# Order of the first loads in a four-layer kernel: x of batch 0 with the first four tiles of weights, the other batches of x last

## What is computed

```python
qk = x @ qk_w.T
vg = x @ vg_w.T
q, k = (qk[..., :KEY_DIM], qk[..., KEY_DIM:])
v, g_out = (vg[..., :VAL_DIM], vg[..., VAL_DIM:])
q = _causal_dwconv_silu(q, q_conv_w)   # the same for k and v
beta = _sigmoid(x @ b_w.T + b_bias + beta_bias) * 2.0
g = -jnp.exp(A_log) * jax.nn.softplus(x @ a_w.T + dt_bias)
o = _gated_delta_rule(q, k, v, g, beta)
o = o * jax.lax.rsqrt(jnp.mean(o * o, axis=-1, keepdims=True) + eps)
o = o * silu(g_out)
x = _layernorm(x + o @ o_w.T)
```

## Time and profile before

| | us |
|---|---|
| median of three runs | 2795.45 |
| lowest and highest | 2789.07, 2799.66 |
| the profiled execution, its time | 2794.95 |
| its span, first to last instruction | 2793.2 |
| TensorE busy | 2512.8 (90%) |
| VectorE busy | 1856.1 (66%) |
| GpSimd busy | 1384.0 (50%) |
| ScalarE busy | 1258.0 (45%) |

### The profile page before, as it was taken

How to read it: one execution, slowest core, us unless ns; L and a number is a source line. 1 busy time by engine, 2 the same in 40 slices (tenths; PEclk the granted TensorE clock), 3 DMA queues, 4 the chain that set the end, 5 groups by cost and what they waited for, 6 DMA issues and landing times.

```text
span 2793.2 us, 33262 instructions
## 1 busy us (share of the span) xinstructions
PE 2512.8 (90%) x11786; PEld 1467.7 (53%) x11786; DVE 1856.1 (66%) x2240; ACT 1258.0 (45%) x1997; POOL 1384.0 (50%) x741
## 2 busy tenths in 40 slices
PE   5999939999989999989678899989989888999998
PEld 2455624444677888855233333333433333677776
DVE  4678875554555666665579789889978888722223
ACT  3443205531223666434456655764665452334333
POOL 0222338860040000241299999999999996122221
PEclk9999759998989999999889899999999999999999
DMA  6443683432053777641275676587587565100000
GB/s 223 140 121 102 87 112 88 95 94 105 12 216 128 256 261 259 208 125 51 84 186 160 173 210 182 162 202 217 170 204 213 174 194 191 46 1 16 15 1 31
DMA packets 278967, 384.98 MB, mean 138 GB/s; under 512 B 127104, under 2 KB 148608, under 8 KB 271392
## 3 DMA queue, kind: packets, MB, share of 16 engines
q1 hardware_dynamic: 268944, 335.77, 41.4%
q0 software_dynamic: 9296, 38.80, 5.7%
q10 hardware_dynamic: 576, 8.39, 0.7%
HBM read 312.91 MB, written 59.51 MB: 133 GB/s over the span
## 4 chain that ended last, share of the span: by engine, by line
PE 55%; POOL 15%; DVE 11%; issue 6%; SPq 5%; DMA 4%; ACT 4%; another core or an unknown queue 0%; PEldq 0%; ACTq 0%; DVEq 0%; POOLq 0%; PEld 0%
POOL arena L786 8%; PE psum L2036 8%; POOL arena L792 5%; PE psum L1983 4%; PE psum L2217 4%; PE psum L2218 4%; PE psum L2832 4%; SPq L2293 4%; PE psum L3019 2%; PE psum L2190 2%; PE psum L2191 2%; PE psum L483 2%; PE psum L2823 1%; PE psum L1879 1%; PE psum L2082 1%
## 5 line engine op out<-in xcount | busy, mean ns | idle before, releaser
L786 POOL TENSOR_TENSOR arena<-arena 128x1024 f32<-128x1024 f32 x256 | 626.3, 2466 | 130.9 <-DVE arena L1551 82.7
L2036 PE MATMUL psum<-arena,cst 128*128 128x512 f32 x1024 | 507.4, 631 | 101.4 <-POOL arena L792 90.4
L1090 ACT ACTIVATE psum<-arena,negA 128x512 f32<-128x512 f32 x512 | 333.4, 682 | 319.0 <-DVE arena L1566 276.4
L2036 PEld LDWEIGHTS psum<-arena,cst 128*128 128x128 f32 x1024 | 189.3, 197 | 400.7 <-issue 215.2
L1566 DVE TENSOR_TENSOR_SCAN arena<-psum,arena 128x512 f32<-128x512 f32 x256 | 310.6, 1213 | 58.8 <-ACT psum L1090 37.6
L1566 DVE TENSOR_TENSOR_SCAN psum<-psum,arena 128x512 f32<-128x512 f32 x256 | 298.7, 1212 | 57.8 <-POOL arena L786 55.0
L792 POOL TENSOR_TENSOR arena<-arena 128x1024 f32<-128x1024 f32 x128 | 312.7, 2443 | 3.0 <-DVE arena L1566 3.0
L840 POOL TENSOR_TENSOR arena<-arena 128x512 f32<-128x512 f32 x64 | 92.3, 1442 | 324.2 <-ACT arena L1214 299.2
L1983 PE MATMUL psum<-arena 128*128 128x512 f32 x512 | 231.8, 596 | 1.3 <-PE psum L1983 0.8
L2381 POOL TENSOR_TENSOR arena<-arena,cst 128x512 f32<-128x512 f32 x64 | 76.3, 1216 | 270.2 <-DVE arena L2685 178.9
L2369 POOL TENSOR_TENSOR arena<-arena,cst 128x1024 f32<-128x1024 f32 x96 | 184.8, 1953 | 43.2 <-PE psum L2933 25.9
(11 more groups left out here) (373 smaller groups left out, 5000.7 us busy)
## 6 DMA issues: line engine op xcount, KB each, us to landing
arena<-bc_scr SPq DMA_DIRECT2D x256, 512.0 KB, 5.4
arena<-w_exp SPq DMA_DIRECT2D x23, 1408.0 KB, 6.1
arena<-in_gu SPq DMA_DIRECT2D x48, 512.0 KB, 4.6
arena<-in_inw SPq DMA_DIRECT2D x32, 512.0 KB, 4.4
arena<-in_dn SPq DMA_DIRECT2D x31, 512.0 KB, 6.9
x_scr<-arena SPq DMA_DIRECT2D x19, 512.0 KB, 5.9
arena<-in_x SPq DMA_DIRECT2D x8, 1024.0 KB, 11.6
w_exp<-in_gu SPq DMA_DIRECT2D x16, 512.0 KB, 7.1
```

The source lines that it names most:

```text
L786: nc.gpsimd.tensor_tensor(dB[:, k % 4], du[:, j:j + 2], BC[:, k % RING, 0].unsqueeze(1).broadcast_to([P, 2, T]), ALU.mult).then_inc(s["db_ ...
L1090: nc.scalar.activation(psum[:, bank], dt[:, b % 2, j + t], ACT.Exp, scale=negA2[:, at:at + 1]).then_inc(s["da_ok"], 1)
L2036: ins = mm(psum[:, t], ident, dB[:, k % 4, t], start=False, stop=(n == NS - 1), skip_group_check=True)
```

## The change

SP issues x of batch 0 right behind the constants, then the three parts of the weights. x of batch 0 and the first part of the weights raise `xload`, the other two parts raise `wload`. SP then waits for the constants and issues x of batches 1 to 3, which raise `consts`, up to 64. TensorE waits for `xload` at 32 ahead of batch 0, for `wload` at 32 ahead of tile 4 of batch 0, and for `consts` at 64 ahead of the later batches and of their gate rows. The bases of the semaphores' second names follow.

```diff
-                ("stt_ok", "std_ok", B), ("vd_ok", "rinv_ok", B), ("ab_in2", "xload", 64), ("ab_in3", "wload", 48),
+                ("stt_ok", "std_ok", B), ("vd_ok", "rinv_ok", B), ("ab_in2", "xload", 32), ("ab_in3", "wload", 32),
...
-                ("w_in0", "m_in", 128 * B), ("w_in1", "t_out", 128 * B), ("xr_in0", "xload", 64 + 96),
-                ("xr_in1", "wload", 48 + 96), ("tg_in0", "ab_in0", 96), ("tg_in1", "ab_in1", 96), ("tg_in2", "v_in1", 128),
+                ("w_in0", "m_in", 128 * B), ("w_in1", "t_out", 128 * B), ("xr_in0", "xload", 32 + 96),
+                ("xr_in1", "wload", 32 + 96), ("tg_in0", "ab_in0", 96), ("tg_in1", "ab_in1", 96), ("tg_in2", "v_in1", 128),
...
         @block.sync
         def _(sp):
             sp.dma_start(cst[:], a["cst"]).then_inc(s["consts"], 16)
-            for c in range(3):
-                sp.dma_start(wproj[:, 4 * c:4 * c + 4], a["wproj"][:, 4 * c:4 * c + 4]).then_inc(s["wload"], 16)
-            for b in range(B):
-                sp.dma_start(xin[:, :, b * T:(b + 1) * T], a["x"][:, :, b * T:(b + 1) * T]).then_inc(s["xload"], 16)
+            sp.dma_start(xin[:, :, 0:T], a["x"][:, :, 0:T]).then_inc(s["xload"], 16)
+            for c, done in enumerate(("xload", "wload", "wload")):
+                sp.dma_start(wproj[:, 4 * c:4 * c + 4], a["wproj"][:, 4 * c:4 * c + 4]).then_inc(s[done], 16)
+            sp.wait_ge(s["consts"], 16)
+            for b in range(1, B):
+                sp.dma_start(xin[:, :, b * T:(b + 1) * T], a["x"][:, :, b * T:(b + 1) * T]).then_inc(s["consts"], 16)
             sp.wait_ge(s["ini"], 5)
...
             pe.wait_ge(s["consts"], 16)
-            pe.wait_ge(s["wload"], 48)
...
             for b in range(B):
-                pe.wait_ge(s["xload"], 64)
+                pe.wait_ge(s["consts"], 16 * B) if b else pe.wait_ge(s["xload"], 32)
                 xb = xin[:, :, b * T:(b + 1) * T]
 
                 def proj(c, bank, done):
+                    if b == 0 and c == 4:
+                        pe.wait_ge(s["wload"], 32)
...
                     pe.wait_ge(s["ini"], 8)
+                    if b:
+                        pe.wait_ge(s["consts"], 16 * B)
                     ring_wait(pe, "r", b, 0)
```

## The result

The changed kernel takes 2780.01 us in the median of 11 runs (2772.44 to 2789.80), the kernel before 2792.85 in the median of 11 (2784.93 to 2800.83). The ratio is 0.9955, 95% interval 0.9938 to 0.9973: 12.6 us less, between 7.5 and 17.3. That is within 0.5% by a little. 2780.01 lies 1.5 us under the forecast of 2781.5, and that closeness is partly luck: the kernel before came out 2.6 us lower over 11 runs (2792.85) than over the three that the forecast started from (2795.45), and the gain 1.1 to 1.3 us smaller than 13.9.

The account below looks back on a forecast made before the run. TensorE's chain bounds the kernel, its first matmul idle 25.1 us until the last load of x. The earlier start gives 13.9 us, all other terms 0: 2795.45 less 13.9 is 2781.5 us, range 2775.5 to 2788.

Parts of the forecast that it names:

- Rival A: The forecast itself: all 13.9 us gained at TensorE's first matmul reach the end of the kernel; 78%.
- Part 1: TensorE's first wait: with loads reordered, gate rows start at 11.2 instead of 25.07 us, gaining 13.9 (12.7 to 14.3).
- Parts 2 and 3: Tile 4's weight wait is met with 14 us spare; SP's wait leaves late x 50 us spare; no cost.
- Part 4: Added wait instructions on TensorE: all met beside matmuls in flight, between 0 and 0.3 us, taken as 0.
- Part 5: TensorE's clock: low-clock spells, about 2 us and one a batch, follow idle stretches and move along at unchanged cost.
- B: Queued early loads are served side by side, so TensorE starts at 16.1; 8.9 us gained, 2786.5; 3%.
- C: Low-clock spells fall differently over the attention stage: two more give 2785.5 (7%), two fewer 2777.5 (8%).
- D and E: Unmoved later work, such as SP's zero writes, absorbs the gain (2795, 2%); or batch 1's x arrives late (2809, 2%).

Follow-up runs that it names:

- weights ahead of x: Changed kernel's waits kept, but all three parts of the weights issued before x of batch 0; ratio 0.9971 to the kernel before.
- first weights, x: Changed kernel with only the first part of the weights issued before x of batch 0; ratio 0.9952 to the kernel before.
- gate rows on x alone, nine matmuls ahead: Kernel whose gate rows wait only for x of batch 0, plus nine unused matmuls on the constants before that wait; ratio 0.9960 to the kernel before.
- small constants first: Against the changed kernel: last 380 constant columns load before x, the rest after the first weights; gate rows wait only for x; 2787.49 us, ratio 0.9939.
- The first experiment: Changed kernel's load order kept, but TensorE again waits for all eight loads before its first matmul; 2795.55 us, ratio 1.0007 to the kernel before.

## Why the prediction was right

The kernels in the order of their start. The third column is 1 - (25.07 - start) / 2793, the start alone carried one for one to the end:

| kernel | first gate matmul | by the start | measured ratio |
|---|---|---|---|
| all waits back | 25.14 | 1.0000 | 1.0007 (0.9996 to 1.0017) |
| weights ahead of x | 16.34 | 0.9969 | 0.9971 (0.9960 to 0.9982) |
| changed | 12.54 | 0.9955 | 0.9955 (0.9938 to 0.9973) |
| changed, again | 11.64 | 0.9952 | 0.9939 (0.9915 to 0.9963) |
| first weights, x | 11.61 | 0.9952 | 0.9952 (0.9934 to 0.9970) |
| changed, late x | 11.25 | 0.9951 | 0.9956 (0.9934 to 0.9979) |
| gate rows on x alone, nine matmuls ahead | 10.62 | 0.9948 | 0.9960 (0.9940 to 0.9980) |
| gate rows on x alone | 9.59, 9.56 | 0.9945, 0.9944 | 0.9942 (0.9929 to 0.9956), 0.9946 (0.9929 to 0.9962) |
| small constants first | 8.84 | 0.9942 | 0.9939 (0.9919 to 0.9959) |

Every interval holds the value by the start. The intervals reach 3 to 7 us to either side and each start is that of one profile, so the table tells 25 from 16, and 16 from 9.6 in one of its two measurements, but not neighbours that are 1 to 3 us apart. **Rival A** was the outcome: what the start gains reaches the end. The first experiment is the plainest ground for it: with the early start taken back the gain is gone.

**Part 1** had the right mechanism and a size that was off. The start was put at 11.2, bounds 10.8 and 12.4; the profiled execution shows 12.54, just outside. The term that was short is the 2.75 us for x of batch 0, measured at 3.9. Over seven profiles with this order the two loads are in at 11.0 to 12.5, and 11.2 is near their early end: six of the seven are later. The sum took a queue that moves the bytes of one load after those of the other, at the pace of one execution. In the changed kernel 84 of the 128 rows of the first weights had moved before x was in. The gain is 12.5 in this profile, not 13.9, and it puts the result on the other side of the 0.5% edge that the text named.

**Parts 2 and 3** held in what they forecast. Their working has two slips on which nothing rests: all eight loads are 8.5 MB, not 8.3, and behind the constants SP has four parts in the queue when it stops, so 4 MB at 6.0 us and not 3. The wait at tile 4 shows nothing; the last x landed at 25.4 (7.3 + 18.1), near the 25 of the forecast; SP's long issue moved to it (5.65 us from 7.28); the zero writes came 0.5 us later, with 31 us of spare left. **Part 4** put the added waits at nothing, and no row shows one; the times could not tell 0.3 us.

**Part 5** was wrong in a sentence that did no harm to the sum: "each follows its own idle stretch, so it moves along with it and costs the same". Spells also follow the 32-column groups, with TensorE busy, and come or stay away between executions of one kernel. The price of about 2 us was near the measured 1.7. The Trainium skill ("TensorE: Matmul & The Clock Gate", Part 1), by which the clock gate does not start with the kernel, describes that scatter better than the forecast's own reading; the two profiles of the changed kernel, 74.9 and 80.0 over one interval, agree with it, and so does it that the length of the gate matmuls at the start (5.26 and 6.24 us) goes with which of the two comes.

**B** fell as an outcome, with the first profile, where the start was 12.54 and not 16.1, and again with weights ahead of x, where x was in only at 16.34 and the first weights had been since 8.6. Its mechanism is there in part: neighbouring loads share the engines, 39 to 84 rows of the first weights ahead of the end of x and 107 behind the small load. **C** is present, as scatter that the medians take out: the span less the start is 2762.1 in the changed kernel's first profile and 2768.1 in the kernel before, and 2763.8 to 2772.9 in the five experiments that ran on chips where the kernel before takes 2793 and that add no matmuls. So the 6.1 us beyond the start are scatter. C looked for it in the attention stage; there the changed kernel's profile lost 2.9 us of its lead, and the expert layer gave 8.2, in a stretch that takes 245.9 to 256.4 us over these profiles. **D and E** have no support: x issued 27 us later still lets nothing wait. No wait took the place of the one removed.

A version that beats the kernel before by more exists: the gate rows on x alone, 0.9942 and 0.9946. That it beats the changed kernel is likely by its start (2 to 3 us), but the intervals overlap.

## What to carry to other kernels

When the first instruction of the bounding engine waits for all loads, count the bytes that it really needs and put those first, each group on a wait of its own. Here the gain was the difference in landing times, 12.6 us for 12.5; the finer wait brought more of it than the order, and the order without the finer wait nothing. Check what becomes late by its distance to its first reader, and spend that distance rather than guard it. Take the duration of an early load from several executions, and count the bytes moved up to its landing: what stands behind it in the queue can take its share.

## What the runs showed that was not expected

The clock fell while TensorE was busy without a break: after 32 matmuls of 32 columns each the following matmuls of 512 columns ran at the lower level for a while, 1.70 us lost each time, in some executions of the same kernel and not in others.

At the start, before the clock is up, the eight gate matmuls took 5.2 to 6.4 us, against 3.6 later, and an earlier start did not always come through: the changed kernel started at 12.54, 11.64 and 11.25 in three profiles (the last with late x), but tile 0 at 17.73, 17.81 and 17.61, and the gate tiles were stored at 72.62, 72.69 and 72.50.

A load of 1 MB early in the queue landed 3.9 us behind its forerunner in one execution of an order and 2.7 in another (9.9 against 8.6 for x of batch 0, with the constants in at 6.0 and 5.9). The loads landed in the order of issue, yet the one behind had already moved 84 of its 128 rows in the first case and 39 in the second.
